# Three of the second batch's six projections moved into the opening's wait for its query parts, with its first high cast and its rotations

## What is computed

```python
q = (x @ Wq).reshape(B, T, H, 2 * DH).transpose(0, 2, 1, 3)      # H = 16, DH = 16
k = (x @ Wk).reshape(B, T, KV, 2 * DH).transpose(0, 2, 1, 3)     # KV = 4
q1, q2 = (q[..., :DH], q[..., DH:]); k1, k2 = (k[..., :DH], k[..., DH:])
# q1, q2, k1, k2 are rotated: o1 = x1*cos - x2*sin, o2 = x1*sin + x2*cos
s1 = einsum('bhtd,bhsd->bhts', q1, k1) * scale + mask            # s2 likewise
diff = softmax(s1) - lam * softmax(s2)
out = einsum('bhts,bhsd->bhtd', diff, v)
```

## Time and profile before

| | us |
|---|---|
| median of 3 timed executions | 858.35 |
| lowest and highest | 858.34, 859.19 |
| the profiled execution | 861.43 |
| its span in the profile | 859.7 |
| busy in the span: PE, DVE, ACT, POOL | 751.9, 465.6, 331.2, 305.4 |

### The profile page before, as it was taken

One profiled execution on the slowest core, in us unless ns is written; L12 is line 12 of the kernel. 1 busy time (PEld: TensorE's weight loads), 2 busy tenths in 40 slices (PEclk: granted clock), 3 DMA queues, 4 the chain that ended last, 5 costly groups with the idle time before them and its releaser, 6 DMA issues.

```text
span 859.7 us, 10350 instructions
## 1 busy us (share of the span) xinstructions
PE 751.9 (87%) x3430; PEld 368.8 (43%) x3430; DVE 465.6 (54%) x1040; ACT 331.2 (39%) x607; POOL 305.4 (36%) x263
## 2 busy tenths in 40 slices
PE   7187899998689989996899899889999798999994
PEld 3142334434234434442344334434425554666662
DVE  2755976761657765516677655467425342334332
ACT  2314534443555333244654332545664012222220
POOL 3028811020983111119831111211240134666653
PEclk9689999999989999997899899999999999999998
DMA  4695074202019310030192100700058012212100
GB/s 127 156 334 138 1 180 80 30 27 38 1 37 184 64 54 5 1 63 1 37 185 40 52 7 1 209 1 1 2 202 293 26 43 59 64 60 61 46 23 1
DMA packets 51748, 62.95 MB, mean 73 GB/s; under 512 B 11303, under 2 KB 42797, under 8 KB 49840
## 3 DMA queue, kind: packets, MB, share of 16 engines
q1 hardware_dynamic: 42992, 49.29, 23.4%
q0 software_dynamic: 3824, 6.83, 2.7%
q10 hardware_dynamic: 4880, 6.16, 2.2%
HBM read 42.59 MB, written 22.41 MB: 76 GB/s over the span
## 4 chain that ended last, share of the span: by engine, by line
PE 71%; DVE 11%; POOL 8%; issue 4%; ACT 2%; DMA 2%; SPq 0%; POOLq 0%; DVEq 0%; ACTq 0%
PE pv_ps L965 15%; PE wide_ps L1043 9%; PE wide_ps L951 7%; PE s_ps L804 7%; DVE mneg L1402 5%; PE wide_ps L792 5%; PE wide_ps L935 4%; PE s_ps L836 3%; PE wide_ps L907 3%; PE s_ps L805 3%; PE pv_ps L1062 2%; PE misc L1062 2%; PE misc L882 2%; POOL work L539 2%; PE wide_ps L940 2%
## 5 line engine op out<-in xcount | busy, mean ns | idle before, releaser
L1402 DVE TENSOR_REDUCE mneg<-s_ps 128x1 f32<-128x384 f32 (+3 forms) x352 | 217.0, 639 | 103.9 <-PE s_ps L805 99.6
L1177 ACT ACTIVATE w_exp<-wide_ps 128x512 f32<-128x512 f32 x320 | 180.2, 599 | 119.0 <-PE wide_ps L951 117.8
L965 PE MATMUL pv_ps<-w_exp,work 128*64 128x512 f32 x640 | 181.7, 647 | 10.0 <-POOL w_exp L1314 8.0
L1314 POOL TENSOR_SCALAR_AFFINE_SELECT w_exp<-w_exp 128x1024 f32<-128x1024 f32 x64 | 70.9, 1109 | 283.6 <-ACT w_exp L1177 283.5
L804 PE MATMUL s_ps<-w_exp 96*128 96x256 bf16 (+3 forms) x512 | 129.8, 313 | 34.3 <-DMA w_exp<-q_parts 18.6
L951 PE MATMUL wide_ps<-w_exp 98*128 98x512 bf16 x320 | 124.1, 397 | 16.3 <-ACT w_exp L1177 14.9
L951 PEld LDWEIGHTS wide_ps<-w_exp 98*128 98x128 bf16 x320 | 31.8, 103 | 159.6 <-ACT w_exp L1177 100.1
L805 PE MATMUL s_ps<-mask,identb 128*128 128x128 bf16 (+2 forms) x352 | 89.0, 253 | 0.0
L1043 PE MATMUL wide_ps<-w_exp,tables 128*128 x184 | 82.8, 592 | 0.0
L804 PEld LDWEIGHTS s_ps<-w_exp 96*128 96x128 bf16 x512 | 46.4, 100 | 82.6 <-DVE mneg L1402 42.4
L1195 ACT COPY work<-pv_ps 128x512 f32<-128x512 f32 x64 | 37.5, 586 | 59.8 <-PE pv_ps L965 59.0
(11 more groups left out here) (164 smaller groups left out, 996.9 us busy)
## 6 DMA issues: line engine op xcount, KB each, us to landing
w_exp<-q_parts SPq DMA_DIRECT2D x96, 128.0 KB, 5.1
w_exp<-w_up_in SPq DMA_DIRECT2D x8, 1024.0 KB, 9.0
slot_tokens<-x ACTq DMA_DIRECT2D x1, 4864.0 KB, 18.5
work<-x_in SPq DMA_DIRECT2D x8, 512.0 KB, 4.3
w_exp<-w_down_in SPq DMA_DIRECT2D x8, 512.0 KB, 9.8
q_parts<-w_exp SPq DMA_DIRECT2D x6, 512.0 KB, 6.7
w_exp<-k_parts SPq DMA_DIRECT2D x18, 128.0 KB, 3.6
gated_rows<-work SPq DMA_DIRECT2D x4, 512.0 KB, 3.1
```

Of the source, the lines that this page charges most:

```text
L965: last = nc.tensor.matmul(pv_ps[s * 64:(s + 1) * 64, :], vo[:, kt, g, :], probs[:, n % NP, s, :], start=(kt == 0), stop=(kt == qt))
L1177: nc.scalar.activation(probs[:, n % NP, s], st_bank(v), ACT.Exp, scale=float(DH) ** -0.5).then_inc(st_done, 1)
L1314: nc.gpsimd.affine_select(out=e, in_=e, compare_op=ALU.is_ge, fill=0.0, base=0, pattern=[[0, 8], [1, P]], channel_multiplier=-1).then_inc( ...
L1402: nc.vector.tensor_reduce(out=mneg[:, qt, rows[0]:rows[-1] + 1], in_=s_ps[:, (v - 1) % 2, 0:len(rows) * w].rearrange("p (r k) -> p r k", r ...
```

## The change

ACT does the first three tasks of HEAD among the start casts: the copy of v ahead of the fourth cast, the two xT copies ahead of the seventh. HEAD is in a new order: all of prep 0 to 4 (two transposes and three projections) come before the first banks, and the remaining three projections stand between groups of four banks of tile 1. A new task `cast_high` lets ACT do batch 1's first high cast in HEAD, behind the copy of prep 6. `PREP_FIRST` puts every operation from `even` of pair 1 on one step sooner, and `casts_at` no longer puts the first high cast into step 0. PE's list follows HEAD, so PE runs prep 0 to 4 right behind v.

```diff
-HEAD = [("v", 0, 0), ("prep", 0, 0), ("prep", 1, 0), ("banks", (0, 0, 8), 0), ("mt", 0, 0)]
-for _k in range(6):
-    HEAD += [("banks", (1, 16 * _k // 6, 16 * (_k + 1) // 6), 0), ("prep", 2 + _k, 0)]
-HEAD.append(("mt", 1, 0))
+HEAD = [("v", 0, 0)] + [("prep", _k, 0) for _k in range(5)] + [
+    ("banks", (0, 0, 8), 0), ("mt", 0, 0), ("banks", (1, 0, 4), 0), ("prep", 5, 0), ("banks", (1, 4, 8), 0), ("prep", 6, 0), ("cast_high", 0, 0),
+    ("banks", (1, 8, 12), 0), ("prep", 7, 0), ("banks", (1, 12, 16), 0), ("mt", 1, 0)]
...
-PREP_FIRST = [-4, -4, -3, -3, -2, -1, -1, 0, 1, 2, 3, 4, 4, 5, 5, 6, 7, 8]
+PREP_FIRST = [-4, -4, -3, -3, -2, -1, -1, -1, 0, 1, 2, 3, 3, 4, 4, 5, 6, 7]
...
-                        if max(prep_step(b, what, pair) + 1, 0) == n:
+                        if prep_step(b, what, pair) >= -1 and prep_step(b, what, pair) + 1 == n:
...
+                if name == "cast_high":
+                    cast(b + 1, 0, arg)
...
-            for part, pair, half in START_CASTS:
+            for i, (part, pair, half) in enumerate(START_CASTS):
+                for name, arg, _ in HEAD[:1] if i == 3 else HEAD[1:3] if i == 6 else []:
+                    task(name, arg, 0)
...
-            for name, arg, _ in HEAD:
+            for name, arg, _ in HEAD[3:]:
                 task(name, arg, 0)
```

## The result

| | before | after |
|---|---|---|
| median of 6 timed executions, same chip | 859.71 | 854.08 |
| lowest and highest | 858.34, 863.37 | 853.29, 856.01 |
| the profiled execution | 861.43 | 854.18 |
| its span | 859.7 | 852.4 |

The ratio is 0.9928, with a 95% interval from 0.99 to 0.9957: 6.2 us faster, between 3.7 and 8.6 (the two medians of the table are 5.6 us apart). The forecast was 9.0 us from the median and 9.3 inside the profiled execution; between the two profiled spans the difference is 7.3. Timed again later, the changed kernel came to a ratio of 0.9917 (0.9889 to 0.9945). These intervals are narrower than the truth: the kernel before, timed against itself, gave 1.0039 (1.0005 to 1.0072), an interval that leaves out 1.

What follows compares the result with a forecast made beforehand. PE, busy 87% of the span, was taken to bound the kernel. Gains of 3.6 + 3.1 + 1.3 + 1.3 = 9.3 us from the 858.35 median gave 849.05, with a 0.3 cost bound 849.3 us; range 845.8 to 855.5.

Steps and rivals of the forecast that it cites:

- the first bank: Sign at the end of the opening: PE's first score bank still comes at 42.5 us.
- POOL's first product: Sign in the head: POOL's first rotation product starts at 43 to 44 us instead of 59.10.
- Part 1: Opening: ACT's copy of v and two xT copies fit its idle time; cost 0, bounds 0 to 0.3 us.
- Part 2: Head: three projections moved into PE's wait shorten DVE's gaps and the split's cast; gain 3.6 us, bounds 1.5 to 4.8.
- Part 3: Body's start: earlier POOL work and high cast end the select's stall, gain 3.1 us, and the low clock behind it, 1.3.
- Part 4: Second to eighth value product: rotations a step sooner cut waits on POOL and DVE; gain 1.3 us, bounds -1.5 to +2.7.
- Rival (a): Body, steps 4 to 8: POOL becomes the bound and value products wait for selects; 4.7 us remain, 853.7; chance 0.20.
- rival (d): Head and steps 0 to 8: eleven DVE operations lose 1.1 us each to POOL; slower, 861.2 us; chance 0.04.
- What is gained stays: From 110 us on: PE is busy 97% and works in the same order, so the 9.3 us gain is kept.
- (b): Opening: xT copies stay behind ACT's stores, so the projections end 11.4 us after the parts; 860.5 us; chance 0.03.
- (c): Early body: third tile's parts land at 78 us, giving back all but 0.8 us; 857.5 us; chance 0.04.
- (e): First tile's banks and body: clock stays high and sooner rotations give all; gain 11.8, 846.5 us; chance 0.09.

Runs made afterwards that it cites:

- e5: The changed kernel plus two more float32 matmuls in PE's wait for the split right before the body; ratio 0.9915 to the kernel before.
- e6: The changed kernel with POOL's rotations and splits from step 0 of batch 0 on made a quarter as long; ratio 0.9881 to the kernel before.
- e3: The changed kernel with all rotations from odd of pair 1 on back in the earlier kernel's steps; ratio 0.9953 to the kernel before.
- e9: The changed kernel with only POOL's last two operations, rest and low of pair 2, in the earlier kernel's steps; 3.8 us faster than the kernel before.

## Why the prediction was right or wrong

The direction and the range held; the size was nearly half as much again as the timed gain (9.0 for 6.2, whose interval ends at 8.6) and 2 us too high against the profile. Of its signs the first bank, POOL's first product and the end of the 3 us wait for an exponential came as said; the body's first scores (69.32 us for 67.5 to 69), the first value product (4.61 us behind them for 4) and above all the eighth (99.87 for 94) came late.

**Part 1**, the copies at no cost: right.

**Part 2**, the head, 3.6 us: 2.67 in the marks (3.35 in the second profile). The term of the gaps was the one that was mis-sized. DVE idles 6.6 us before the 16 maxima where 5.3 was forecast (8.1 before). The first projection was to leave the low clock half way, with a gap of 2.3 us. It didn't: the gap was 3.21, and the banks before it at the low clock added two of 0.27 and 0.44. The split's cast gave 1.13 back for 1.1, and the first cast lost 0.23 for 0.3. Up to that cast the first tile's banks were 0.2 us quicker, which was not in the sum.

**Part 3**, the stall, 3.1 us: 2.49. The mechanism was right, the select was in time. Of the missing 0.6, 0.44 is the clock, since with e5's fill the distance is 4.17; the forecast was 4.0.

**Part 3**, the clock, 1.3 us: -0.12 in the first profile, 1.15 in the second, and the clock was low in both. This step failed: I took the low clock behind the first value product to be a result of the 3 us stall. The runs show it low without that stall, behind PE's 1.3 us wait for the split and the banks in short pieces before it, and high in all three kernels that fill the wait. That the second profile has most of the 1.3 us is where the low stretch fell, not the mechanism of the forecast.

**Part 4**, 1.3 us: -0.33 up to the eighth product. The excess of the combinations did not halve. It stayed, at 2.9 us for 2.6, and e6 shows that it is what lies between 21.4 and PE's own 18.4. Rival (a) had the right place with the wrong mechanism: no value product waited for a select there; PE waited for banks behind DVE, which waited for POOL.

**Not in the sum**: 2.89 us from the eighth to the tenth product. The rows were there: the split in step 8 was among rival (d)'s six operations, but I did not ask where the step sooner would put POOL's last low part. e3 and e9 show it to be the one place where the step sooner pays. The same rows contradict a sentence of part 2, that no row shows the subtraction with POOL beside it: the one in step 8 took 1.02 us, POOL's select beside it. The Trainium skill, GPSIMD Engine Reference, section 1 (Specifications), names instructions with two SBUF inputs, and this trace agrees for the subtraction, which has two; it also names a two-port mode, and no row shows the mode of the cast that waits. In the first split the subtraction took 0.19 as counted, because POOL's last product had just ended.

So 2.67 + 2.49 - 0.12 - 0.33 + 2.89 = 7.60 for 9.3: two terms near, two gone, one found. The found one was luck: the terms that were forecast came to 4.7 of 9.3 us. "What is gained stays" held between the two first profiles, 745.9 us behind the tenth product in both; between the second ones it did not (749.9 for 745.7). Why the medians give 6.2 and not 7.3 stays open; single executions of one kernel on one chip spread over up to 10 us (before, 855.8 to 865.7; after, 850.4 to 857.3), and the part behind the tenth product alone took 742.5 to 749.9 us in the profiles, with the low stretches of the later batches in different places. That is as much as most of the effects above, so their times could not show them. The 0.2% that the prediction called measurable was too small: the same kernel differed from itself by 0.39%.

Of the rivals, (b), (c) and (d) did not come; of (e) the high clock in the first banks came only with a fill.

## What to carry to other kernels

Work moved into a wait is worth what it starved where it stood, not its duration, and only with the schedule behind it does the gain last: here the move alone gave no measurable time and the schedule alone about half (in the traces 2.1 and 4.4 of 7.6 us). When an engine's list is moved by a step, look for every instruction of another engine that it collides with, at the old and at the new place; the largest gain of the step sooner was one collision of 2 us that it missed. Count distances between marks in two profiles of the same kernel before you trust the time of a half per cent.

## What the runs showed of the hardware

- DVE's cast of 32 columns from SBUF waits for the POOL operation that runs (0.18 us alone; 0.41, 1.15, 1.31 and 1.32 beside one in the change, the kernel before and the schedule alone, and 0.99 with the four projections), ending within 0.1 us of its end; the subtraction with two SBUF inputs does so too (0.19 alone, 1.02 beside a select, 2.05 beside POOL's rest). DVE's maxima, which read PSUM, took 0.65 us an instruction beside POOL and without it.
- PE's granted clock fell to the lower level (1.2 GHz) behind stretches in which it worked in short pieces with waits of 0.5 to 1.3 us between them, without any long wait (the change, low from 71.5 us); two more float32 matmuls in a wait of 1.3 us kept it at 2.4 GHz in all three kernels that had them.
- A float32 matmul of 128x512 is listed as two instructions, 0.43 us each at the high clock: a projection, counted above as four matmuls, is two in the code and four in the profile, the 1.88 us of the rows.
- The same program against itself came out 0.39% apart, with a 95% interval (0.05 to 0.72%) that leaves out zero.
